# Half of the stream mixing moved from VectorE to GpSimd, and the causal mask moved from TensorE to VectorE

## What is computed

```python
xn = _layernorm(x)
# layer 0: attention with one head of 128, and a mix of four streams of 128 columns
H_res = (1.0 - g) * I + g * sinkhorn(H_res_logits)           # (b, t, 4, 4)
y = einsum('btnc,btn->btc', x_streams, H_pre) @ W_branch
x_mixed = einsum('btij,btjc->btic', H_res, x_streams)
y_distributed = einsum('btc,btn->btnc', y, H_post)
x = x + attention0(xn) + (x_mixed + y_distributed)
# layer 1: causal attention, 32 query heads in 8 groups of 4 that share keys and values
xn = _layernorm(x)
scores = einsum('bhqd,bhkd->bhqk', q, k) * scale
scores = where(tril, scores, -1e9)
out = softmax(scores) @ v ; x = x + out @ Wo.T + gated_lora_ffn(xn)
```

## Time and profile before

| | |
|---|---|
| time, median of 3 runs | 2548.25 us (2543.29 to 2548.75) |
| the profiled execution | 2546.12 us, its span 2544.3 us |
| busy, share of the span | PE 90%, PEld 71%, DVE 61%, ACT 41%, POOL 36% |
| granted TensorE clock, mean | 0.956 |
| the mix stage's last part, TensorE idle | 286.5 to 380 us |
| the first attention | about 504 to 1440 us |
| the second attention | about 1605 to 2544 us |

### The profile page before, as it was taken

How to read it: one execution, slowest core, us unless ns; L and a number is a source line. 1 busy time by engine, 2 the same in 40 slices (tenths; PEclk the granted TensorE clock), 3 DMA queues, 4 the chain that set the end, 5 groups by cost and what they waited for, 6 DMA issues and landing times. The chain is left out here.

```text
span 2544.3 us, 35763 instructions
## 1 busy us (share of the span) xinstructions
PE 2279.3 (90%) x11666; PEld 1818.9 (71%) x11666; DVE 1551.3 (61%) x3333; ACT 1044.3 (41%) x2182; POOL 917.7 (36%) x957
## 2 busy tenths in 40 slices
PE   5767309799999999999999797899999999999998
PEld 4623107678888888878888685687888888888886
DVE  4289995555656565665656555566565656565665
ACT  3323203344545444444445232344444545454444
POOL 2654214142525243343524101334352525343341
PEclk9879659999999999999999898999999999999999
DMA  9400003801010101010110227201011010101010
GB/s 344 137 0 1 1 35 158 325 31 38 29 49 25 58 8 58 8 58 25 41 50 1 115 92 259 83 9 58 25 41 49 16 49 25 58 8 58 8 46 29
DMA packets 71409, 159.58 MB, mean 63 GB/s; under 512 B 4416, under 2 KB 37568, under 8 KB 64832
## 3 DMA queue, kind: packets, MB, share of 16 engines
q1 hardware_dynamic: 70912, 157.44, 17.8%
q10 hardware_dynamic: 432, 1.32, 0.1%
HBM read 110.52 MB, written 69.99 MB: 71 GB/s over the span
## 5 line engine op out<-in xcount | busy, mean ns | idle before, releaser
L1439 POOL TENSOR_TENSOR probs<-probs,rinv 128x1024 f32<-128x1024 f32 (+7 forms) x384 | 439.1, 1147 | 1117.9 <-DVE rinv L1466 1117.9
L1475 DVE TENSOR_TENSOR pT<-psum,pT 128x512 fp32r<-128x512 f32 x576 | 387.1, 689 | 313.9 <-ACT pT L1515 308.6
L1509 ACT ACTIVATE probs<-psum,nmax 128x256 f32<-128x256 f32 (+7 forms) x512 | 380.7, 743 | 366.9 <-DVE nmax L1461 362.6
L1515 ACT ACTIVATE pT<-psum 128x512 fp32r<-128x512 f32 x576 | 330.3, 595 | 333.3 <-PE psum L1569 332.2
L1461 DVE TENSOR_REDUCE nmax<-psum 128x1 f32<-128x256 f32 (+7 forms) x512 | 378.1, 751 | 48.6 <-PE psum L1558 42.4
L1569 PE MATMUL psum<-ident,probs 128*128 128x128 f32 x2304 | 329.8, 273 | 8.5 <-issue 6.1
L1569 PEld LDWEIGHTS psum<-ident,probs 128*128 128x128 f32 x2304 | 263.2, 141 | 48.5 <-DVE pT L1475 9.0
L93 PE MATMUL psum<-keys,q 128*128 128x512 f32 (+3 forms) x768 | 276.7, 360 | 2.8 <-DVE q L1451 2.8
L93 PE MATMUL psum<-pT,vals 128*128 128x512 f32 x576 | 263.6, 458 | 4.0
L95 PE MATMUL psum<-keys,q 128*128 128x512 f32 (+3 forms) x768 | 262.0, 341 | 0.0
L94 PE MATMUL psum<-keys,q 128*128 128x512 f32 (+3 forms) x768 | 261.7, 341 | 0.0
(11 more groups left out here) (265 smaller groups left out, 3927.1 us busy)
## 6 DMA issues: line engine op xcount, KB each, us to landing
k_parts<-kv_out SPq DMA_DIRECT2D x32, 512.0 KB, 5.1
wq<-wq_copy SPq DMA_DIRECT2D x16, 1024.0 KB, 4.8
wo<-wo_copy SPq DMA_DIRECT2D x16, 1024.0 KB, 4.8
v_parts<-kv_out SPq DMA_DIRECT2D x32, 512.0 KB, 4.0
keys<-k_parts SPq DMA_DIRECT2D x32, 512.0 KB, 4.7
vals<-v_parts SPq DMA_DIRECT2D x64, 256.0 KB, 3.1
acc<-in_x SPq DMA_DIRECT2D x4, 1024.0 KB, 11.9
up_l<-up_copy SPq DMA_DIRECT2D x2, 1024.0 KB, 6.1
```

Source lines behind the costliest of these rows:

```text
L1439: pool.tensor_tensor(p, p, rinv[:, u, h:h + 1].to_broadcast([P, (TB - u) * P]), ALU.mult).then_inc(p_ok, 1)
L1475: dve.tensor_tensor(pT[:, n % PT_SLOTS, 1, :], bank[T_BANK + n % 2], f32(pT[:, n % PT_SLOTS, 0, :]), ALU.subtract).then_inc(t_lo, 1)
L1509: act.activation(probs[:, u % 2, h, 0:n], bank2[2 * (h % 2)][:, off:off + n], ACT.Exp, bias=nmax[:, u, h:h + 1], accum_out=rsum[:, u, h:h ...
L1515: act.activation(pT[:, n % PT_SLOTS, 0, :], bank[T_BANK + n % 2], ACT.Copy).then_inc(t_hi, 1)
```

## The change

Two edits.

**The mix.** In `layer0_mix` VectorE now mixes tiles 0 to 7 alone. SyncE stores the second batch's normalised input and y to DRAM (`xn_s`, `y_s`). The mixing weights `mix` and `rw` are kept in SBUF. In the first batch's attention, GpSimd mixes one tile of the second batch in each of the 8 iterations: it waits for the tile's two loads and then does 5 pairs of instructions of 128x512, a product into `product` and an add into `acc`. One pair follows the normalisation of head 2 of query tiles 2 to 6. GpSimd's loop over the iterations is written out for this batch.

**The mask.** The bf16 matmul is gone. The mask is an fp32 tile, and VectorE adds it in place in PSUM, 128x128, before each maximum, which waits for it. The copies `identb` and `maskb` are gone.

```diff
-            for k in range(0, NT, 2):
+            for k in range(0, TB, 2):
...
+            sp.dma_start(m.xn_s, xn[:, TB:NT, :]).then_inc(later, 16)
+            sp.wait_ge(y_ok, 4)
+            sp.dma_start(m.y_s, y[:, TB:NT, :]).then_inc(later, 16)
+            sp.wait_ge(later, 32)
...
+            def later_loads(t):
+                if t:
+                    sp.wait_ge(mixed, 2 * (NS + 1) * t)
+                sp.dma_start(later_x[:], m.xn_s[:, t, :]).then_inc(later_in, 16)
+                sp.dma_start(later_y[:], m.y_s[:, t, :]).then_inc(later_in, 16)
...
+            if mixes_later:
+                later_loads(0)
             for it in range(ITERS - 1):
                 loads(it, it + 1)
+                if mixes_later:
+                    later_loads(it + 1)
...
+            def mixing(t):
+
+                x = m.acc[:, TB * (b + 1) + t, :].rearrange("p (i c) -> p i c", i=NS)
+                pool.wait_ge(later_in, 32 * (t + 1))
+                for j in range(NS + 1):
+                    n = 2 * ((NS + 1) * t + j)
+                    stream = later_x[:, j * D:(j + 1) * D] if j < NS else later_y[:]
+                    weight = m.mix[:, TB * (b + 1) + t, :, j] if j < NS else m.rw[:, TB * (b + 1) + t, 1, :]
+                    if n:
+                        pool.wait_ge(mixed, n)
+                    pool.tensor_tensor(product[:], stream.unsqueeze(1).to_broadcast([P, NS, D]),
+                                       weight.unsqueeze(2).to_broadcast([P, NS, D]), ALU.mult).then_inc(mixed, 1)
+                    yield
+                    pool.wait_ge(mixed, n + 1)
+                    pool.tensor_tensor(x, x, product[:], ALU.add).then_inc(mixed, 1)
+                    yield
...
+                        if h == REP - 2 and 2 <= u:
+                            next(beside, None)
+                            next(beside, None)
...
                         dve.wait_ge(s_mm, it * SC + (REP * u + h + 1))
+                        diagonal = bank2[2 * (h % 2)][:, off + n - P:off + n]
+                        dve.tensor_tensor(diagonal, diagonal, m.mask[:], ALU.add).then_inc(s_masked, 1)
+                        dve.wait_ge(s_masked, it * SC + (REP * u + h + 1))
                         dve.tensor_reduce(nmax[:, u, h:h + 1], bank2[2 * (h % 2)][:, off:off + n], AX.X, ALU.max,
                                           negate=True).then_inc(s_max, 1)
...
-
-                        pe.matmul(slot[:, off + n - P:off + n], m.identb[:], m.maskb[:], start=False, stop=True).then_inc(s_mm, 1)
+                        ins.then_inc(s_mm, 1)
```

More of the change, by code:

```diff
@@ L169, in _ @@
             pool.memset(m.ident[:], 0.0).then_inc(const, 1)
-            pool.memset(m.maskb[:], 0.0).then_inc(const, 1)
+            pool.memset(m.mask[:], 0.0).then_inc(const, 1)
             pool.memset(m.ones[:], 1.0).then_inc(const, 1)
@@ L177, in _ @@
                                base=0, pattern=[[-1, P]], channel_multiplier=1).then_inc(const, 1)
-            pool.affine_select(out=m.maskb[:], in_=m.maskb[:], compare_op=ALU.is_ge, fill=MASKED,
+            pool.affine_select(out=m.mask[:], in_=m.mask[:], compare_op=ALU.is_ge, fill=MASKED,
                                base=0, pattern=[[-1, P]], channel_multiplier=1).then_inc(const, 1)
-            pool.wait_ge(const, 7)
-            pool.tensor_copy(m.identb[:], m.ident[:]).then_inc(const, 1)
             pool.wait_ge(wq_hi, 1)
@@ L308, in _ @@
         def _(pe):
-            pe.wait_ge(const, 8)
+            pe.wait_ge(const, 7)
             def turn_x(n):
@@ L368, in layer0_mix @@
         PARTS = 2
-        Z, K, T = (sb(n, [P, NT, NS, NS]) for n in ("sk_z", "sk_k", "sk_t"))
+        Z, K = (sb(n, [P, NT, NS, NS]) for n in ("sk_z", "sk_k"))
+        T, rw = m.mix, m.rw
         sm, row, col, lrow, lcol, u, v = (sb(n, [P, NT, NS]) for n in ("sk_s", "sk_row", "sk_col", "sk_lr", "sk_lc", "sk_u", "sk_v"))
-        rw = sb("rw", [P, NT, 2, NS])
         rws, rwm = sb("rw_s", [P, NT, 2]), sb("rw_m", [P, NT, 2])
@@ L383, in layer0_mix @@
         xn, x1 = m.xn0, m.acc
-        w_in, gate_ok = sem("b_w_in"), sem("b_gate")
+        w_in, gate_ok, later = sem("b_w_in"), sem("b_gate"), sem("b_later")
         chain, chain_act = sem("b_chain"), sem("b_chainact")
@@ L1220, in layer1_attention @@
         o_hi, o_lo, w_mm, x_add = (sem("e_" + n) for n in ("o_hi", "o_lo", "w_mm", "x_add"))
-        stored = sem("e_stored")
+        stored, s_masked = sem("e_stored"), sem("e_s_masked")
+        mixes_later = b < B - 1
+        if mixes_later:
+            later_x, later_y, product = sb("later_x", [P, HID]), sb("later_y", [P, D]), sb("product", [P, NS, D])
+            later_in, mixed = sem("e_later_in"), sem("e_mixed")
         ITERS = KV_HEADS
@@ L1425, in _, with body @@
             pool.memset(free[:, 3:4], 0.0).then_inc(x_add, X0)
-            def body(it, last):
+            def mixing(t):
[13 more added lines that the diff above has]
+                    yield
+            def body(it, last, beside=iter(())):
                 for kind, *arg in steps(last):
@@ L1439, in body @@
                         pool.tensor_tensor(p, p, rinv[:, u, h:h + 1].to_broadcast([P, (TB - u) * P]), ALU.mult).then_inc(p_ok, 1)
-            with pool.Fori(0, ITERS - 1) as it:
-                body(it, False)
-            body(ITERS - 1, True)
+                        if h == REP - 2 and 2 <= u:
+                            next(beside, None)
+                            next(beside, None)
+                for _ in beside:
+                    pass
+            if mixes_later:
+                for it in range(ITERS):
+                    body(it, it == ITERS - 1, mixing(it))
+            else:
+                with pool.Fori(0, ITERS - 1) as it:
+                    body(it, False)
+                body(ITERS - 1, True)
         @block.vector
@@ L1554, in body @@
                         for lo, hi in cuts:
-                            mm3(pe, slot[:, off + lo:off + hi], [(q[:, 0, h, qs], q[:, 1, h, qs], keys[:, 0, lo:hi], keys[:, 1, lo:hi])],
-                                stop=hi < n)
-                        pe.matmul(slot[:, off + n - P:off + n], m.identb[:], m.maskb[:], start=False, stop=True).then_inc(s_mm, 1)
+                            ins = mm3(pe, slot[:, off + lo:off + hi],
+                                      [(q[:, 0, h, qs], q[:, 1, h, qs], keys[:, 0, lo:hi], keys[:, 1, lo:hi])])
+                        ins.then_inc(s_mm, 1)
                     elif kind == "turn":
@@ L1622, in program @@
         m.ident, m.ones, m.zero = consts("ident", [P, P]), consts("ones", [P, P]), consts("zero", [P, 1])
-        m.identb, m.maskb = consts("identb", [P, P], BF16), consts("maskb", [P, P], BF16)
+        m.mask = consts("mask", [P, P])
         kept = Column(nc, KEPT, 207.8)
@@ L1626, in program @@
         m.allowed = kept("allowed", [P, TOPK, EXP])
+        m.mix, m.rw = kept("mix", [P, NT, NS, NS]), kept("rw", [P, NT, 2, NS])
         def internal(name, shape):
@@ L1641, in program @@
         m.tmp_s = internal("tmp_parts", (P, S))
+        m.xn_s, m.y_s = internal("xn_later", (P, TB, HID)), internal("y_later", (P, TB, D))
         m.ffn_in, m.ffn_hi, m.copied = (ctx.enter_context(nc.semaphore(n)) for n in ("ffn_in", "ffn_hi", "copied"))
```

## The result

| | before | changed |
|---|---|---|
| time, median (4 runs each) | 2548.28 us | 2502.32 us (2499.52 to 2507.14) |
| ratio, 95% interval | | 0.9826 (0.9806 to 0.9845) |
| profiled execution, span | 2546.12, 2544.3 us | 2502.25, 2500.1 us |
| DVE, POOL busy | 61%, 36% | 67%, 41% |
| mix, to the next stage's first instruction | 84.4 us | 42.4 us |

Faster by 46 us where 75 were forecast; the time lies just above the range. The mix gave what it should. The 16 iterations together gave nothing: -9 us in the 14 that repeat (the first seven of each batch), +9 us in the two last ones.

What follows compares the result with a forecast made beforehand. TensorE's own instructions were taken to bound the 16 attention iterations, plus its idle stretch during the mix. 2546.12 - 42.0 - 52.6 + 17.6 + 2 = 2471.1 us profiled, so 2473 us expected, range 2453 to 2499.

Steps and rivals of the forecast that it cites:

- The mix, -42.0 us: Mix before the attention: half of VectorE's 84.1 us goes, saving 42.0 us, as the next stage waits for nothing else.
- GpSimd's half: First batch's attention: GpSimd mixes 8 tiles, some 11.6 us per iteration in free time, nothing on TensorE's path by itself.
- The mask matmul, 3.3 us per iteration: TensorE in the attention: removing 32 mask matmuls frees 3.3 us per iteration, 52.6 us over 16.
- The rival by which it was nearly free: Mask matmul: next product's weights are exposed elsewhere, only 26 us gained instead of 52.6; 2500 us, chance 0.06.
- The masking add, 0.29 us: VectorE's 128x128 add in PSUM: 0.29 us each, bounds 0.285 and 0.347, plus 0.03 wait before the maximum.
- Together 1.1 us per iteration: Attention iterations: later maxima from the add make TensorE stop 1.1 us more per iteration, +17.6 us over 16.
- Its two places: No margin at tile 1's transposes, 0.32 us later, and tile 2's product, about 0.35 us later.
- In tiles 3 to 7 ... 0.4 us: Margins of 0.4 to 0.5 us used up by the delay and TensorE's gain; estimated 0.4 us per iteration.
- all latency hidden: Rival: the adds fit in between and TensorE's stops only move earlier; 2455 us, chance 0.12.
- I take 0.25 us per iteration in the first batch, +2 us: GpSimd's mixing and VectorE's head 3 normalisation hold each other up: 0.25 us per first-batch iteration, +2 us.
- GpSimd blocks head 3: Rival: each pair makes VectorE wait a whole instruction, transposes late; put at 2490 us, bound 2525, chance 0.12.
- The rival on the other side: Slower: the add costs TensorE 0.32 us at each of 512 heads, +69 us, 2617 us; chance of slower 0.03.

Runs made afterwards that it cites:

- the mix alone: Changed kernel with the mask matmul back on TensorE, GpSimd still mixing the second batch: 2508.75 us, ratio 0.9849 to the kernel before.
- without any mask: Changed kernel with the masking add removed and no mask at all: 2464.36 us, ratio 0.9672.
- the split: Changed kernel, VectorE adding the mask for tile 0 and heads 0 and 1 of tiles 1 to 6, TensorE the rest; GpSimd's pairs wait for head 3: 2477.72 us.
- complement: Changed kernel, VectorE adding the mask only for heads 2 and 3 of tiles 1 to 6, TensorE the rest; GpSimd's pairs wait for head 3: 2515.02 us.
- the experiment in which the pairs wait: Changed kernel with each pair of GpSimd's mixing instructions held back until VectorE has normalised head 3: 2491.43 us, ratio 0.9785.
- the mask alone: Changed kernel with VectorE mixing all 16 tiles as before, the mask still added by VectorE: 2531.55 us, ratio 0.9942.
- the last iteration on TensorE: Changed kernel with the mask a TensorE matmul again in the last iteration of each attention: 2497.34 us, ratio 0.9805.
- the kernel with three tiles on TensorE: Changed kernel, mask matmul kept for heads 2 and 3 of tiles 1 to 3 and the last iteration, 26 adds on VectorE, GpSimd's pairs waiting: 2494.44 us.
- the version with five tiles: Changed kernel, mask matmul kept for heads 2 and 3 of tiles 1 to 5 and the last iteration, 22 adds on VectorE, GpSimd's pairs waiting: 2478.40 us.
- the later maximum: Changed kernel with head 3's masking add and maximum in tiles 2 to 6 one step later, behind the next pT subtraction: 2552.5 us, ratio 1.0021.

## Why the prediction was wrong

- *The mix, -42.0 us.* Right to the hundredth: 84.09 to 42.09 us between its first instruction and its last, and nothing in its place.
- *GpSimd's half.* Right in price (1.05 and 1.26 to 1.30 us) and in that it costs the iterations nothing: with the mix alone, 115.94 us.
- *The mask matmul, 3.3 us per iteration.* Right in the repeated iterations: 3.0 us without any mask, 3.3 net of the stops. The rival by which it was nearly free falls. For all 16 it was too much: from the mix alone to no mask are 44 us, not 52.6, as the two last iterations gave 0.8 us together instead of 6.6.
- *The masking add, 0.29 us.* Right.
- *"Together 1.1 us per iteration".* This is the first term that failed: 2.3 us measured in batch 1. Its two places were right in mechanism and size (0.33 and 0.39 us), but they weren't the only ones without a margin: TensorE stopped for 0.37 us at tile 3's last product before the change too, and for 0.83 at the group's end. The term "In tiles 3 to 7 ... 0.4 us" measured 1.6. I had read those margins as single delays of one add; the rows show two adds in a row, coupled by the reciprocal of head 2 in VectorE's order, and new stops in tiles 4 and 5 and at the group's end, where there had been none or smaller ones. The split and its complement show that heads 2 and 3 carry these costs; the coupling by the reciprocal is read from the rows, and no run moved it. "VectorE and ScalarE are free 40% of the time" was no argument, and as a rival (all latency hidden) it fell too.
- *"I take 0.25 us per iteration in the first batch, +2 us".* In the repeated iterations nearly right for TensorE, 0.45 us by the experiment in which the pairs wait, and so was the margin behind it: VectorE waits for 0.2 to 1.1 us in each of tiles 4 to 6. It failed in the last iteration, which I had priced like the others. There is less work between the normalisation and the transposes there, the wait is 1.1 us, TensorE stands for 2.3 us, and its clock falls afterwards (5.7 us, for which the sum had no term). I had named the mechanism as a rival ("GpSimd blocks head 3"). That its 17 us are near the 11 us that the wait gave is luck: the rival counted 40 pairs, and most of the cost came in one iteration and by the clock.
- *The sum.* The forecast was 2471.1 us for the profiled execution. From 2471.1 to the profiled 2502.25 us are 31 us. The 14 repeated iterations gave 9 us instead of 14 x 2.06 = 28.9: 20 us. The last two cost 9 us instead of giving 4: 13 us, nearly half of it the clock. The start of the mix (287.14 instead of 290.16) and the other stages gave back 2 us.
- *The rival on the other side* needed 0.185 us per head. All the adds and what they brought cost 2.3 / 32 = 0.07 us. For heads 2 and 3 alone it comes near: the 12 adds of the complement brought 4.35 - 2.28 = 2.1 us, 0.17 each, above the 0.095 that a matmul costs.

What stays open: how the 1.6 us divide between the reciprocal's wait and the fuller queue at the group's end, and why the stops at the group's end grow by 0.24 us even with no mask. The iterations of batch 1 take 114.9 us with the mask alone and 114.8 with the last iteration on TensorE, against 115.1 here and where the pairs wait, for the same work. In the latter two, tile 3's normalisation or GpSimd's L108 is longer, the one by 0.9 to 1.1 or the other by 0.36 us, in the former L108 by 0.25; that this is the reason wasn't tried apart.

## What to carry to other kernels

An instruction moved off the bounding engine is to be priced twice: what it frees (the distance from start to start with and without it, which held here to 0.1 us in a repeated iteration, but not in the last ones), and what it puts into each chain that ends in a wait of that engine. Follow such a chain over every loop step, with what stands ahead in the queue of the helping engine; one delay may hold up the next. Loop ends and last iterations are to be read by themselves, since they have less work to cover a wait; where two engines can meet at a port, a wait that keeps the less urgent one back may be worth more than either instruction; and work that moves between engines can be split by instance, to keep the gain where there is slack.

## What the runs showed of the hardware

**Who comes first at the shared port.** The prediction said that VectorE gets in when GpSimd's running instruction ends. In the changed kernel VectorE's normalisation starts first by the rows, and still waits for all of GpSimd's:

```profile
1753.03 1.69 DVE L1516 TENSOR_SCALAR probs<-probs,rinv 128x640 f32<-128x640 f32 x1
1753.07 1.30 POOL L108 TENSOR_TENSOR wq<-wq 128x512 fp32r<-128x512 f32 x1
...
2098.48 0.55 DVE L1516 TENSOR_SCALAR probs<-probs,rinv 128x640 f32<-128x640 f32 x1
2098.53 1.66 POOL L108 TENSOR_TENSOR wq<-wq 128x512 fp32r<-128x512 f32 x1
```

At 2098.48 it takes 0.55 us, its time when alone, with GpSimd's L108 starting 0.05 us later, and there GpSimd's takes 1.66 us instead of 1.3. So within 0.05 us either can win. VectorE lost 1.14 us to GpSimd's 1.30, GpSimd 0.36 us to VectorE's 0.55. The Trainium skill ("SBUF — State Buffer", section Who interferes with whom) says that whoever issues first gets the pair and the other is blocked fully. The first pair nearly agrees with the full block; the start times in the rows don't tell who was first.

**Instruction fetches in a loop.** In the kernel with three tiles on TensorE, VectorE stands at the start of an iteration of batch 1, six times, for nothing that the profile shows, in front of the first add and the first maximum. Its waits (sum, times, longest), and its queue of instruction fetches:

```profile
DVE psum L1520 <- issue: 20.4, 6, 3.9
...
DVE nmax L1522 <- issue: 13.9, 6, 2.4
```

```profile
q14 instruction: 64, 0.52, 0.1%
```

The other versions have 31 to 34 packets on that queue (the changed kernel: "q14 instruction: 33, 0.27, 0.0%") and no such wait. Of the 64, 35 fall into these iterations, two of them into the 8 us around one of the waits; the version with five tiles has 8 in all from 1500 us on. TensorE's scores then start 1.3 us late in the iteration looked at, and the seven iterations take 815.1 us (111.6 to 119.1 each) instead of 799.1 in batch 0, 16 us more. Four adds fewer (the version with five tiles) and it is gone. That the fetches cause it is my reading; it wasn't tried apart.

**The clock.** The stops of 0.2 to 0.9 us in the repeated iterations of the changed kernel left the granted clock at 1.00. Behind longer ones it was sometimes lower, and the length of the stop doesn't tell when. In the last iteration of batch 0, stops of 2.26 and 2.15 us in the changed kernel were followed by 0.64 and 0.50 over the next 4 us. With the mix alone, stops of 1.90 and 2.07 us in the same iteration were followed by 1.00. With the later maximum, a stop of 1.88 or 1.89 us came in ten iterations, and in seven of them the clock behind it was 0.57 to 0.65, in the other three 1.00. What makes the difference isn't known from these runs. Where it did fall, it cost more (5.7 us in the changed kernel's last iteration of batch 0) than the longer stops before it (2.4).
